# First norm, first products and edge counting in one function, with the edges counted in pairs of blocks

## What is computed

```python
x = x + _L0_gnn_ref(_layernorm(x), edge_index, W1, ...)     # x: 1250 x 768
...
h = (x @ W.T).reshape(n, heads, out_ch)                     # W1: 1024 x 768, 8 heads of 128
a_src = jnp.einsum('nhc,hc->nh', h, att_src)
a_dst = jnp.einsum('nhc,hc->nh', h, att_dst)
e = leaky_relu(a_src[src] + a_dst[dst], 0.2)
m = segment_max(e, dst); ex = jnp.exp(e - m[dst])
alpha = ex / (segment_sum(ex, dst)[dst] + 1e-16)
out = segment_sum(alpha[:, :, None] * h[src], dst) + bias   # 41250 edges, sorted by dst
...
x = x + _L0_ffn_ref(_layernorm(x)[None], phi, w1, b1, w2, b2)[0]
```

## Time and profile before

| | us |
|---|---|
| median of 3 runs | 1963.15 (1962.36 to 1964.62) |
| the profiled execution's own time | 1967.12 |
| its span, from the first to the last instruction | 1965.3 |
| PE busy (matmuls) | 1727.5 (88%) |
| DVE busy | 1144.2 (58%) |
| ACT busy | 861.4 (44%) |
| POOL busy | 266.0 (14%) |
| mean granted TensorE clock | 0.964 |

### The profile page before, as it was taken

One profiled execution on the slowest core, in us unless ns is written; L12 is line 12 of the kernel. 1 busy time (PEld: TensorE's weight loads), 2 busy tenths in 40 slices (PEclk: granted clock), 3 DMA queues, 4 the chain that ended last, 5 costly groups with the idle time before them and its releaser, 6 DMA issues. The chain is left out here.

```text
span 1965.3 us, 30827 instructions
## 1 busy us (share of the span) xinstructions
PE 1727.5 (88%) x9896; PEld 1000.6 (51%) x9896; DVE 1144.2 (58%) x1762; ACT 861.4 (44%) x1345; POOL 266.0 (14%) x115
## 2 busy tenths in 40 slices
PE   3947877767999998979999699999999996999799
PEld 2423333335565564645554355656555654666455
DVE  6776777778998984643232145555555565665311
ACT  3106767768888872720111033333333333655200
POOL 0000000008887851300000000000000000000000
PEclk9978999998999998989999899999999998999899
DMA  5110000001121224021100022111122114441411
GB/s 206 40 34 1 0 0 0 0 0 23 32 35 46 33 19 138 1 73 49 41 33 17 32 67 81 63 63 63 63 74 74 63 48 145 131 122 36 147 64 46
DMA packets 49615, 108.35 MB, mean 55 GB/s; under 512 B 16526, under 2 KB 18664, under 8 KB 49420
## 3 DMA queue, kind: packets, MB, share of 16 engines
q1 hardware_dynamic: 49484, 107.38, 17.8%
q10 hardware_dynamic: 64, 0.08, 0.0%
HBM read 79.02 MB, written 28.43 MB: 55 GB/s over the span
## 5 line engine op out<-in xcount | busy, mean ns | idle before, releaser
L672 PE MATMUL ce_c<-one_src,one_dst 128*128 x1053 | 211.6, 347 | 44.1 <-issue 38.2
L773 POOL TENSOR_TENSOR base<-s_row,ln_c 128x1250 f32<-128x1250 f32 x80 | 227.5, 2845 | 56.0 <-DVE top L828 55.3
L615 DVE TENSOR_SCALAR one_src<-iota,src 128x1280 f16 x351 | 170.8, 550 | 71.1 <-PE ce_c L672 64.5
L90 PE MATMUL di_l<-x2t_hi,ph_hi 128*128 128x512 f16 (+1 forms) x576 | 196.7, 341 | 12.8 <-DVE ph_lo L1415 11.4
L91 PE MATMUL di_l<-x2t_lo,ph_hi 128*128 128x512 f16 (+1 forms) x576 | 196.6, 341 | 0.0
L92 PE MATMUL di_l<-x2t_hi,ph_lo 128*128 128x512 f16 (+1 forms) x576 | 196.6, 341 | 0.0
L897 PE MATMUL at_o<-pt,h 128*128 128x384 f32 (+1 forms) x480 | 185.2, 523 | 0.0
L672 PEld LDWEIGHTS ce_c<-one_src,one_dst 128*128 x1053 | 101.7, 97 | 154.1 <-issue 93.6
L639 ACT ACTIVATE apart<-iota,minus_dst 128x128 f16 x351 | 115.4, 391 | 72.6 <-PE ce_c L672 39.1
L884 PE MATMUL at_t<-ident,q 128*128 128x128 f32 x800 | 107.7, 284 | 31.9 <-ACT q L807 31.2
L90 PE MATMUL co_c<-ps_hi,hid_hi 128*128 128x305 f16 (+1 forms) x384 | 114.8, 299 | 21.3 <-DVE ps_lo L1642 20.8
(11 more groups left out here) (237 smaller groups left out, 3306.2 us busy)
## 6 DMA issues: line engine op xcount, KB each, us to landing
logits_t<-lg SPq DMA_DIRECT2D x32, 625.0 KB, 3.7
logits_in<-logits_t SPq DMA_DIRECT2D x32, 625.0 KB, 4.1
phf<-in_phi SPq DMA_DIRECT2D x32, 384.0 KB, 3.9
s_row<-a_rows SPq DMA_DIRECT2D x9, 640.0 KB, 5.8
ew1f<-in_fw SPq DMA_DIRECT2D x6, 768.0 KB, 5.0
wf<-in_fw SPq DMA_DIRECT2D x12, 384.0 KB, 6.9
xs<-in_x SPq DMA_DIRECT2D x10, 384.0 KB, 7.3
res<-in_x SPq DMA_DIRECT2D x10, 384.0 KB, 3.1
```

The costliest lines, as they stand in the source:

```text
L90: eng.matmul(out, lh, rh, start=first, stop=False, skip_group_check=True)
L615: eng.tensor_scalar(one_src[:, ds(slot + i, 1), :], const["iota"][:, :], src[:, ds(block_at + i, 1)], None, ALU.is_equal)\
L672: mm = eng.matmul(cp[:, j % 2, a:a + n], one_dst[:, ds(slot + i, 1), :], one_src[:, ds(slot + i, 1), a:a + n], start=False, stop=False, sk ...
L773: eng.tensor_tensor(base[:, k % 2, 0:N], s_row[:, head % 2, 0:N], ln_c[:, j, 0:N], ALU.add)\
```

## The change

The three functions become one, `first_stage`, in one block. The edges are loaded first and their bounds found ahead of the products. The norm is taken tile by tile, two tiles ahead of the products. The last tile's copy and weighing (L620, L524) and the transposing of the sums come behind the loops of row tiles 0, 0 and 1 of the counting. `x` has four buffers in place of ten, and the parts of the weights are loaded one by one.

Counting takes two blocks in a pass of the loop, with a ring of four; a row tile with an odd number of blocks gets one more, in which no edge has its destination in the tile. The matmuls of a block have 226, 512 and 512 columns in this order, where they had 512, 512 and 256. PE reads one bound for a row tile, DVE and ACT two. The logarithm is taken of twice the count plus 2^-25, straight from PSUM, and one operation on DVE (L550) makes of it what L599, L602 and L606 made.

```diff
 CHUNKS = ((0, 512), (512, 512), (1024, N - 1024))
+CHUNKS_COUNTED = ((1024, N - 1024), (0, 512), (512, 512))
...
+NONE = 2.0 ** -25
+NONE_TIMES = MASK / 17.0
...
-    norm_and_turn(nc, mem, sem, const, "ln1", x, xt, w1, w1t.rearrange("(k p) c -> p k c", p=P),
...
-    node_products(nc, mem, sem, const, xt, w1, in_w1, att1, h, nad1, scratch["a1"], w2t, att2, v2)
...
-    count_edges(nc, mem, sem, const, edges, ln_c, s_row1, in_s, scratch["a1"], bias_col, in_bias, gb1)
+    first_stage(nc, mem, early, sem, const, x, edges, w1t, att1, w2t, att2, gb1, h, nad1, scratch["a1"], s_row1,
+                in_s, bias_col, in_bias, v2, ln_c)
...
+    XS, XT, BLOCKS, PAIR = 4, 3, 4, 2
+    EBP = EB + 1
+    ETP = EBP * BLOCK
...
+    with nc.psum_tensor("fs", [P, 8, BANK], F32) as banks, nc.Block() as block:
+        x_out = banks[:, 0:2, :].rearrange("p b n -> p (b n)")
+        small = banks[:, 2, :]
+        a_out = banks[:, 7, :]
...
+        def h_out(t):
+            return banks[:, 3 + 2 * (t % 2):5 + 2 * (t % 2), :].rearrange("p b n -> p (b n)")
+
+        def counts(j):
+            at = 3 * (j % 2)
+            return banks[:, at:at + 3, :].rearrange("p b n -> p (b n)")
...
+        def spans(eng, shifts):
...
+            first = 0
+            for j in range(NT):
+                last = eng.value_load(bounds[0:1, 0, j:j + 1], min_val=1, max_val=NT * EBP // 2)
+                shift = eng.value_load(bounds[0:1, 1, j:j + 1], min_val=-NT * EBP, max_val=EB) if shifts else None
+                yield j, first, last, shift
+                first = last
...
+        def slot(pair, n):
+            return (pair % 2) * PAIR * BLOCK + n * BLOCK
...
+            eng.dma_start(raw[:, :, :], edges).then_inc(in_edges, 16)
+            load_x(0)
+            load_x(1)
+            stored_w1 = w1t.rearrange("(k p) c -> p k c", p=P)
+            for k in range(KD):
+                if k:
+                    eng.wait_ge(in_w1, 16 * k)
+                eng.dma_start(w1f[:, k, :], stored_w1[:, k, :]).then_inc(in_w1, 16)
+            load_x(2)
+            load_x(3)
+            eng.dma_start(att[:, :, :], att1.unsqueeze(0).to_broadcast([P, 2, C1])).then_inc(in_att, 16)
+            eng.wait_ge(prep, 5)
+            eng.dma_start(attb[:, :, :], att2.unsqueeze(0).to_broadcast([P, 2, D])).then_inc(in_w2[0], 16)
+            eng.dma_start(w2f[:, :, :], w2t.rearrange("(k p) c -> p k c", p=P)).then_inc(in_w2[1], 16)
+            for t in range(XS, NT):
+                load_x(t)
...
+            def weigh(t):
+                eng.wait_ge(h_read, t + 1)
+                if t == 0:
+                    eng.wait_ge(in_att, 16)
+                else:
+                    eng.wait_ge(a_done, t)
+                eng.tensor_tensor(weighted[:, :, :], h_out(t).unsqueeze(1).to_broadcast([P, 2, C1]),
+                                  att[:, :, :], ALU.mult).then_inc(weighted_ready, 1)
+                eng.wait_ge(weighted_ready, t + 1)
+                eng.tensor_reduce(a_all[:, t, :], weighted[:, :, :].rearrange("p s (h c) -> p (s h) c", c=P),
+                                  AX_X, ALU.add).then_inc(a_done, 1)
...
+            def finish(j):
+                eng.wait_ge(ln_ready, j + 1)
+                eng.scalar_tensor_tensor(ln_c[:, j, :], lns[:, j % 2, :], NONE_TIMES, lns[:, j % 2, :],
+                                         ALU.mult, ALU.min).then_inc(out_ready, 1)
...
+            ranks_of_tiles()
+            moments(0)
+            moments(1)
+            nodes_of_edges()
+            norm(0)
+            farthest()
+            norm(1)
+            for k in range(KD):
+                eng.wait_ge(wt_hi, k + 1)
+                eng.scalar_tensor_tensor(wt[1][:, k, :], w1f[:, k, :], S_WEIGHT, wt[0][:, k, :],
+                                         ALU.mult, ALU.subtract).then_inc(wt_lo, 1)
+                if k == 1:
+                    low_x(0)
+                if k == 3:
+                    bounds_of_tiles()
+            moments(2)
+            for t in range(NT):
+                if t + 1 < NT:
+                    low_x(t + 1)
+                if t + 2 < NT:
+                    norm(t + 2)
+                if t + 3 < NT:
+                    moments(t + 3)
+                if t >= 1:
+                    weigh(t - 1)
+                if 1 <= t <= KC:
+                    second_weights(t - 1)
+            eng.wait_ge(v2_ready, 2 * KC)
+
...
+            for j, first, last, shift in spans(eng, True):
+                with eng.Fori(first, last) as pair:
+                    for n in range(PAIR):
+                        eng.wait_ge(free, PAIR * pair + n + 1)
+                        at = block_columns(PAIR * pair + n, shift)
+                        for i in range(BLOCK):
+                            eng.tensor_scalar(one_src[:, ds(slot(pair, n) + i, 1), :], const["iota"][:, :],
+                                              src[:, ds(at + i, 1)], None, ALU.is_equal).then_inc(src_ready, 1)
+                if j == 0:
+                    weigh(NT - 1)
+                    logits()
+                if j == 1:
+                    eng.wait_ge(v2_hi, 1)
+                    eng.scalar_tensor_tensor(v2[1][:, :, :], v2f[:, :, :], S_TURN, v2[0][:, :, :],
+                                             ALU.mult, ALU.subtract).then_inc(v2_lo, 1)
+                if j >= 1:
+                    finish(j - 1)
+            finish(NT - 1)
+            eng.wait_ge(out_ready, NT)
+            eng.wait_ge(v2_lo, 1)
+            eng.wait_ge(a_read, 2)
...
+            def log(j):
+                eng.wait_ge(count_done, j + 1)
+                if j >= 2:
+                    eng.wait_ge(out_ready, j - 1)
+                eng.activation(lns[:, j % 2, :], counts(j)[:, 0:NP], ACT.Ln, bias=const["none"][:, 0:1], scale=2.0)\
+                   .then_inc(ln_ready, 1)
...
+            deviation(0)
+            deviation(1)
+            for k in range(KD):
+                eng.wait_ge(in_w1, 16 * (k + 1))
+                eng.activation(wt[0][:, k, :], w1f[:, k, :], ACT.Copy, scale=S_WEIGHT).then_inc(wt_hi, 1)
+                if k == 1:
+                    high_x(0)
+            deviation(2)
+            for t in range(NT):
+                if t + 1 < NT:
+                    high_x(t + 1)
+                if t >= 1:
+                    read_h(t - 1)
+                if t + 3 < NT:
+                    deviation(t + 3)
...
+            for j, first, last, shift in spans(eng, True):
+                with eng.Fori(first, last) as pair:
+                    for n in range(PAIR):
+                        eng.wait_ge(free, PAIR * pair + n + 1)
+                        at = block_columns(PAIR * pair + n, shift)
+                        for i in range(BLOCK):
+                            eng.activation(apart[:, n, i, :], const["iota"][:, j * P:(j + 1) * P],
+                                           ACT.Abs, bias=minus_dst[:, ds(at + i, 1)]).then_inc(apart_ready, 1)
+                        eng.wait_ge(apart_ready, (PAIR * pair + n) * BLOCK + BLOCK)
+                        eng.activation(one_dst[:, ds(slot(pair, n), BLOCK), :], apart[:, n, :, :],
+                                       ACT.Relu, bias=const["one"][:, 0:1], scale=-1.0).then_inc(dst_ready, 1)
+                if j == 0:
+                    read_h(NT - 1)
+                if j == 1:
+                    eng.activation(v2[0][:, :, :], v2f[:, :, :], ACT.Copy, scale=S_TURN).then_inc(v2_hi, 1)
+                if j == 2:
+                    eng.wait_ge(a_turn, 1)
+                    eng.activation(a_turned[:, :], a_out[0:HEADS * NT, 0:P], ACT.Copy).then_inc(a_kept, 1)
+                if j >= 1:
...
+            def turn_x(t):
+                eng.wait_ge(normed_ready, t + 1)
+                if t >= 1:
+                    eng.wait_ge(x_lo, t)
...
+            def product(t):
+                eng.wait_ge(x_lo, t + 1)
+                if t >= 2:
+                    eng.wait_ge(weighted_ready, t - 1)
+                    eng.wait_ge(h_read, t - 1)
...
+            eng.wait_ge(prep, 5)
+            eng.transpose(small[0:2 * NT, 0:P], ends[:, :], const["ident"][:, :]).then_inc(ends_turned, 1)
+            turn_x(0)
+            eng.wait_ge(top_ready, 1)
+            eng.transpose(small[0:1, P:P + 2 * NT], top[:, :], const["ident"][0:2 * NT, 0:2 * NT])\
+               .then_inc(top_turned, 1)
+            turn_x(1)
+            for t in range(NT):
+                product(t)
+                if t + 2 < NT:
+                    turn_x(t + 2)
...
+            for j, first, last, _ in spans(eng, False):
+                if j == 1:
+                    eng.wait_ge(weighted_ready, NT)
+                if j >= 2:
+                    eng.wait_ge(ln_ready, j - 1)
+                if j == 2:
+                    eng.wait_ge(a_read, 1)
+                    eng.transpose(a_out[0:HEADS * NT, 0:P], a_src[:, :, :].rearrange("p h t -> p (h t)"),
+                                  const["ident"][:, :]).then_inc(a_turn, 1)
```

(17 more changed lines are left out.)

533 lines of the change are left out of this document (204 added, 329 removed).

## The result

| | before | after |
|---|---|---|
| median, us | 1963.84 (1962.36 to 1964.62) | 1895.79 (1894.35 to 1898.86) |
| span of the profiled execution, us | 1965.3 | 1893.6 |
| mean granted TensorE clock | 0.964 | 0.974 |
| first counting matmul, us | 157.19 | 122.08 |
| closing matmuls of the last row tile, us | 433.44 | 365.58 |

The changed kernel is faster. The ratio is 0.9648, with a 95% interval of 0.9633 to 0.9662, and the difference of the medians is 68.05 us. The span is 71.7 us shorter. 69.4 of this lie ahead of the next function. The other 2.3 us lie behind it, where nothing was changed, and a second profile of the changed kernel spans 1896.8 us with the next function at 369.80, so I count them as scatter.

What follows compares the result with a forecast made beforehand. DVE's norms, then PE's products, a 35.4 us hole and counting bound by PE's instruction stream were taken as limits. Terms of 32.7, 31.7 and 1.5 us sum to 65.9, from 1963.15 to 1897 us; 8 in 10 for 1878 to 1914.

Steps and rivals of the forecast that it cites:

- up to the first counting matmul: First stage: edges' work early, norm merged into products, DVE limiting at 9.5 us a tile; counting starts 32.7 us earlier.
- the counting: Counting loop: 59 passes of 3.99 us and cheaper changes of row tile make 244.5 us, 31.7 us less.
- the end: After the last closing matmuls: a logarithm and one operation replace three DVE operations, 1.5 us less.
- Rival (c): First stage: handing over between engines costs a microsecond more a tile, giving 1906 us; chance 0.12.
- the middle gap: PE's idle time between a pass's two blocks: between nothing and 0.77 us, 0.51 by number of instructions.
- Rival (a): Counting: the gap inside a pass is as long as the loop's, 4.36 us a pass, 1919 us; chance 0.13.
- (b): Counting: the gap inside a pass vanishes, covered by long matmuls, 3.59 us a pass, 1873 us; chance 0.12.
- A change of row tile: Counting: cost 2.0 us more than a pass; with two loads of bounds gone on PE, 0.78 is left.
- The cover of the last weighing: Behind row tile 0's loop: 4.5 us on DVE, covered by a ring of four blocks, some 8 us; 0.7 lost.
- The irregular passes: Counting: 3.2 us of irregular passes before the change, half carried over, 1.4 in the sum.
- The chunks: Counting: matmul order and 30 fewer columns worth nothing while the instruction stream limits; 0.04 us a block if it were hidden.
- Rival (d): Counting: doubled loop bodies make an engine wait for instructions, 2.0 us a pass, 2015 us, slower than before; chance 0.03.

Runs made afterwards that it cites:

- e5: Changed kernel with the two sums over the second layer's weights cut to 64 of 768 columns: ratio 0.9647, first counting matmul at 119.56 us against 122.08.
- e6: Changed kernel with the edges' ranks and bounds moved back behind the products: ratio 0.9744, first counting matmul at 141.57 us against 122.08.
- e10: e6 with the load of x's fifth tile issued ahead of the second layer's weights: ratio 0.9730, first counting matmul at 135.78 us.
- e3: Changed kernel with a block's matmuls in the old order and width, 512, 512, 256 columns: ratio 0.9646, next function at 366.55 us against 369.79.
- e1: Changed kernel with one block in a pass of the counting loop, no block added: ratio 0.9752, next function at 391.38 us against 369.79.
- e2: Changed kernel with two more, unused loads of bounds per row tile on PE: ratio 0.9710, next function at 380.10 us against 369.79.
- e11: Changed kernel with a block's matmuls in the order 512, 512, 226 columns: ratio 0.9626, next function at 365.87 us against 369.79.
- e9: e4 with a block's matmuls in the order 512, 512, 226 columns: ratio 0.9450, next function at 333.57 us.
- e7: Changed kernel with the old three operations from counts to logarithm at the end: ratio 0.9670, next function at 371.31 us against 369.79.
- e4: Changed kernel with four blocks in a pass and constant places in the ring: ratio 0.9465, next function at 334.16 us against 369.79.
- e8: e4 with a register holding zero added to every place in the ring: ratio 0.9596, next function at 359.98 us.

## Why the prediction was right

The forecast was 1897 us; 1895.79 were measured, 1.2 us less. Part of this is luck: the terms were 3.5 us too small in sum, and the profiled span fell by 71.7 us where the medians fell by 68.05. The three terms against the trace:

| term | predicted | measured |
|---|---|---|
| up to the first counting matmul | 32.7 less | 35.1 less (157.19 to 122.08) |
| the counting | 31.7 less | 32.7 less (276.2 to 243.5) |
| the end | 1.5 less | 1.6 less (5.79 to 4.21) |
| sum | 65.9 | 69.4 |

**First stage.** The mechanism was right step by step: the edges' work goes into the start, where the weights are still arriving, and then DVE is the limit without a rest. `low_x(2)` was put at 44.8 and is at 43.75, a tile at 9.5 and is 9.25, and PE's idle at 0.9 and is 0.67 where it comes. These allowances, 1.1 us and six tiles of 0.25, make 2.6 us, and the term was too small by 2.4. e5 shows that a tile of DVE is 0.82 us longer than one of PE, where I had 0.85, though both are shorter than I put them. But PE's idle time came in three tiles only, not in each: PE began with a lead, which DVE used up, and both end together, DVE at 119.12 and PE at 119.33. So a shorter tile of DVE alone wins 2.5 us (e5), where I had put PE as the limit throughout at 4. Rival (c), a microsecond lost in each handing over, has nothing in the trace. e6 and e10 show the other half: some 12 us of the ranks' work cost nothing early, since DVE would wait for the weights then.

**Counting.** A pass was put at 3.99 us and is 3.98. The gap inside was 0.40 by my choice between 0 and 0.77; it is 0.34, and the loop's end keeps 0.79. The 0.06 us that the middle gap is shorter went elsewhere: the two bodies together are 2.85 us, not 2.82, and the loop's end is 0.02 longer. The loads came in threes with 0.16 us between them, not in nines as I had said. In the old order (e3) they do come in nines, the gaps are 0.75 and 0.32, and a pass is 3.92. So two errors cancelled, a middle gap put too long and an order of chunks put at nothing. Rival (a), equal gaps, and (b), none, are both refuted by the alternating rows. The figure of the Trainium skill for a compare-and-branch (Advanced Engine Details and Errata, Control Flow Timing), by which the gap would have been some 0.53, is small beside what a loop's end adds here: 0.45 us for the branch and the loop's register operation together. e1 confirms the pairs' share, e2 that of the loads of bounds. A change of row tile adds 0.63 us to the passes (24.51 less 6 times 3.98), not 0.78. For ACT I wrote 22.6 us a row tile; 12 times 1.72 and a logarithm of 1.3 are 21.9, which changes nothing.

Two small terms of the sum were off. **The cover of the last weighing**: I gave 0.7 us for it, and row tile 1 lost 2.9 (27.4 us against 24.5). I had laid four blocks of the ring against 4.5 us of DVE. But from 139.45, where DVE begins to wait for ACT's copy, to 147.33, where it makes matrices again, it is 7.9 us, and the 1.42 and 1.45 us of idle time in them were not in my sum. **The irregular passes**, 1.4 us carried over from before, are 0.8: two row tiles take 24.9 us. In sum: 59 times 3.98 is 234.8, nine changes 5.7, row tile 1 2.9 and the irregular ones 0.8, which is 244.2. 243.5 were measured, since this count begins with the first counting matmul and so leaves out the opening of row tile 0, some 0.7 us (222.37 to 223.03 in a later one).

**The chunks.** "The order of the chunks and the 30 columns less are worth nothing while the instruction stream is the limit, and I cost them at nothing" is the one step whose reasoning failed. The columns are as said (0.7 us). The order costs 3.9 us (e11), and only where the stream is the limit (e9).

**The end** came out as predicted, and e7 measures it alone: 1.52 us.

**Rival (d)**, a stall for instructions at each pass, did not come: in the counting the idle times that end with "issue" are at most 0.31 us on DVE, but for the 1.45 at 147.33, and ACT has none. That one stands where DVE reads two bounds, and the 2.00 of the earlier trace rows where it read three. At the 0.65 us that a load costs PE (e2) they would be 1.3 and 2.0, which fits, though no run changes DVE's loads alone. And e4, whose body is twice as long, has no gap on PE for a whole row tile. So the stall that the Trainium skill describes for taken branches (Runtime: NRT & Kernel Launch, Instruction fetch mechanics) does not show in this loop. The limit of the changed kernel is still PE's instruction stream, though the profile's row names ACT for most of the idle time. The passes are 3.98 us apart whether the row names ACT or "issue", ACT itself waits 0.50 us a pass for PE, and two edits that touch PE alone move the end of the counting, e2 by 10.3 us and e11 by 3.9.

## What to carry to other kernels

Where idle time of a few tenths ends with "issue" once in a loop, look first at operands whose address comes from a register, and then at the loop's end: with four blocks in a pass the ring's places became constants, and this was worth 25.8 us, the fewer loop ends 9.8. An engine's time for a piece of work in such a loop is not its own limit as long as its addresses come from registers too. Work that needs nothing but its own data belongs where another load is being waited for, and when it is moved, the place of each load in the queue has to be followed as well.

## What I had not expected of the hardware

- Constant addresses made ACT faster too, not PE alone. From 200 to 300 us, its four operations for a block took 1.64 to 1.80 us in the changed kernel, with 0.20 us ahead of L656 once a pass, 1.62 to 1.89 in e8, and 1.52 to 1.59 in e4, with a few of 1.68.
- The same nine matmuls in another order changed a pass by 0.07 us under a register-addressed stream, and by nothing in e4 and e9. Why is open.
- A load of a bound into a register costs PE about 0.65 us between two row tiles (e2), more than the gap between the two blocks of a pass (0.34) and less than that at the loop's end (0.79).
- Behind a rest of 4.80 us of PE, e4 counted for some 3 us at a granted clock of 0.50 and lost 2.0 us by it. The kernel before lost nearly nothing by the same clock in its first blocks (11.0 us for five, against 10.9). That the stream's gaps left room for this is my reading.
